# Splitting the two feed-forward weight loads of a Mamba2 + SwiGLU layer into six pieces with semaphores of their own

## What is computed

```python
xn = layernorm(x)
# attn branch: mixer (not shown), then a SwiGLU with float32 weights, 2752 wide
h  = xn + mamba2_mixer(rmsnorm(xn))
a  = h + (silu(rms(h) @ gate_w.T) * (rms(h) @ up_w.T)) @ down_w.T
# ffn branch: a SwiGLU with int32 weights scaled by 1/127, 3072 wide
f  = (silu(xn @ wg.T) * (xn @ wu.T)) @ wd.T
out = x + a + f
```

## Time and profile before

| | us |
|---|---|
| time, median of 2 runs | 4552.88 |
| the 2 runs | 4582.55 and 4523.2 |
| profiled execution, its own time | 4524.84 |
| its span, slowest core (core 5) | 4523.1 |
| spans of the 8 cores | 4493.2 to 4523.1 |
| PE busy in the span | 2282.1 (50%) |
| DVE busy in the span | 1812.8 (40%) |

### The profile page before, as it was taken

The page is one execution under the profiler, slowest core; times in us unless marked ns, Lnnn a source line. Parts: engine busy times, 40 slices in busy tenths (PEclk is TensorE's granted clock), DMA queues, the critical chain, the costliest instruction groups (busy, mean ns, idle before and its releaser), DMA issues.

```text
span 4523.1 us, 36356 instructions; the slowest of 8 cores (4493.2 to 4523.1 us)
## 1 busy us (share of the span) xinstructions
PE 2282.1 (50%) x9681; PEld 1012.9 (22%) x9681; DVE 1812.8 (40%) x3925; ACT 559.7 (12%) x1011; POOL 149.6 (3%) x152
## 2 busy tenths in 40 slices
PE   0526603438850334343433322777776706878877
PEld 0212201213320111111111111333333302333333
DVE  3532495653139565656565640222222201222222
ACT  3000020000122221212121110111111000000000
POOL 0110000000000000000000000000000000000000
PEclk9998755559975555555555556788888758988988
DMA  6552000011120311111111136000000081111111
GB/s 163 190 156 59 19 0 1 1 40 22 53 59 0 84 66 38 61 42 57 47 52 50 49 79 108 19 19 24 24 19 19 15 158 44 49 33 33 49 33 35
DMA packets 85968, 234.08 MB, mean 52 GB/s; under 512 B 23856, under 2 KB 24656, under 8 KB 85136
## 3 DMA queue, kind: packets, MB, share of 16 engines
q0 software_dynamic: 32128, 106.44, 10.2%
q1 hardware_dynamic: 51344, 116.94, 8.4%
q10 hardware_dynamic: 2304, 8.39, 0.5%
HBM read 235.13 MB, written 51.66 MB: 63 GB/s over the span
## 4 chain that ended last, share of the span: by engine, by line
PE 43%; DVE 21%; issue 15%; DMA 9%; ACT 5%; another core or an unknown queue 5%; DVEq 1%; SPq 0%; ACTq 0%; POOL 0%; POOLq 0%
PE P L1057 4%; PE P L1207 4%; PE P L1211 4%; PE P L930 3%; PE P L1061 3%; PE P L420 3%; PE P L425 3%; DMA bcast<-lam_dram 3%; DMA wbuf<-w_in 3%; DVE Emt L845 2%; PE P L1246 2%; PE P L1098 2%; PE PS L1246 2%; PE P L645 2%
## 5 line engine op out<-in xcount | busy, mean ns | idle before, releaser
L851 PE MATMUL P<-x_tok,Emt 128*128 128x64 bf16 x512 | 108.4, 212 | 293.8 <-DVE Emt L845 278.9
L549 DVE SCALAR_TENSOR_TENSOR B_acc<-xbc,c_convw,B_acc 128x2048 bf16<-128x2048 bf16 x108 | 245.3, 2344 | 0.0
L1228 DVE TENSOR_TENSOR F_h<-F_h,P 128x1024 bf16<-128x1024 bf16 x48 | 58.6, 1221 | 436.0 <-ACT F_h L1222 436.0
L1207 PE MATMUL P<-wg,F_xf 128*128 128x512 bf16 x384 | 146.3, 381 | 164.8 <-DMA wd2b<-w_d 119.9
L836 ACT ACTIVATE Est<-Est 128x128 f32<-128x128 f32 x512 | 156.5, 310 | 432.4 <-DVE Est L830 430.9
L332 PE MATMUL P<-c_identf,A_n 128*128 128x128 f32 x256 | 90.6, 445 | 197.9 <-DVE A_n L320 166.2
L1078 DVE TENSOR_TENSOR E_h<-E_h,P 128x1024 bf16<-128x1024 bf16 (+1 forms) x48 | 53.3, 1110 | 336.9 <-ACT E_h L1072 336.9
L1057 PE MATMUL P<-wg,E_hnT 128*128 128x512 bf16 x384 | 146.3, 404 | 65.8 <-ACT E_h L1072 65.4
L845 DVE SCALAR_TENSOR_TENSOR Emt<-Est,dtk,Gm 128x128 bf16<-128x128 f32 x512 | 175.8, 346 | 9.1 <-PE P L851 6.5
L830 DVE TENSOR_SCALAR Est<-bcast,lam_tok 128x128 f32<-128x128 f32 x512 | 152.5, 303 | 54.0 <-DMA bcast<-lam_dram 4.3
L645 PE MATMUL P<-c_identf,dt 32*128 32x32 f32 x32 | 8.9, 278 | 321.1 <-issue 161.5
(11 more groups left out here) (198 smaller groups left out, 4278.1 us busy)
## 6 DMA issues: line engine op xcount, KB each, us to landing
bcast<-lam_dram SPq DMA_DIRECT2D x64, 512.0 KB
A_x<-x_own SPq DMA_DIRECT2D x32, 512.0 KB, 3.8
A_x<-x_pre SPq DMA_DIRECT2D x32, 512.0 KB, 4.2
wd<-w_d POOLq DMA_DIRECT2D x2, 5376.0 KB, 102.9
xn_dram<-A_n POOLq DMA_DIRECT2D x16, 512.0 KB, 4.6
xfh<-xfp_dram SPq DMA_DIRECT2D x4, 2048.0 KB, 14.3
sz_dram<-zst POOLq DMA_DIRECT2D x32, 256.0 KB, 2.3
sz_t<-sz_dram POOLq DMA_DIRECT2D x16, 512.0 KB, 3.9
```

The source lines that it names most:

```text
L549: e.scalar_tensor_tensor(a[:, :], xbc[:, ec * CW + k:ec * CW + k + T], self.c["convw"][:, ec * 4 + k:ec * 4 + k + 1], a[:, :], ALU.mult, A ...
L1207: e.matmul(slots[j][:, 0:512], xft[p][:, dc * 128:(dc + 1) * 128], w[:, dc * INTER2 + cb:dc * INTER2 + cb + 512], start=(dc == 0), stop=(d ...
```

## The change

In both phases the loads of gate and up are split by the column parts that the matmuls use, and issued in the order in which tile 0 needs them: gate part 0, up part 0, gate part 1, and so on. These six loads take semaphores in turn from the list `dw, dl0, dl1, dp, dw, dl0`. A load whose semaphore is already in use makes GpSimd wait until the earlier load on it has landed. The down load follows on `dl1` and the rest of down on `dp`, with the same kind of wait. TensorE's wait at the head of the phase is gone. In its place, in tile 0 alone, each of the six gate and up groups waits for its own piece, and the first down matmul waits for both down loads. The bytes loaded and the places they go to stay the same. What computes stays the same.

The part for E; the one for F is the same with 3 parts of 1024 columns and the `wg2, wu2, wd2, wd2b` tiles:

```diff
-        ldg = self.op("gpsimd", lambda e: e.dma_start(
-            bass.AP(wg1, 0, [[NDC * INTER1, 128], [INTER1, NDC], [1, INTER1]]),
...
-            inc=("dw", 16), wait=[("st", self.cnt["st"])])
...
-        self.wait("tensor", "dw", lddb)
+        EPARTS = [(0, 1024), (1024, 1024), (2048, 704)]
+        wsem = ["dw", "dl0", "dl1", "dp", "dw", "dl0", "dl1", "dp"]
+        t_wg, t_wu = {}, {}
+        si = 0
+        first = [("st", self.cnt["st"])]
+        lastw = {}
+        for pi, (cb, cn) in enumerate(EPARTS):
+            for wdst, wsrc, td in ((wg1, self.w_g1, t_wg), (wu1, self.w_u1, t_wu)):
+                s = wsem[si]
+                w = first + ([(s, lastw[s])] if s in lastw else [])
+                tok = self.op("gpsimd",
+                    lambda e, wdst=wdst, wsrc=wsrc, cb=cb, cn=cn: e.dma_start(
+                        bass.AP(wdst, cb, [[NDC * INTER1, 128], [INTER1, NDC], [1, cn]]),
+                        bass.AP(wsrc.tensor, cb,
+                                [[INTER1, 128], [128 * INTER1, NDC], [1, cn]])),
+                    inc=(s, 16), wait=w)
+                td[pi] = (s, tok)
+                lastw[s] = tok
+                first = []
+                si = (si + 1) % len(wsem)
+        t_wd = ("dl1", self.op("gpsimd", lambda e: e.dma_start(
...
+            inc=("dl1", 16), wait=[("dl1", lastw["dl1"])]))
+        t_wdb = ("dp", self.op("gpsimd", lambda e: e.dma_start(
...
+            inc=("dp", 16), wait=[("dp", lastw["dp"])]))
...
                             wait=(([("sa", t_silu_u.get(uu - 1)), ("sv", t_hnt[i])]
-                                   if j == 0 else [("sv", t_spu.get(uu - 1))])
+                                   if j == 0 else [("sv", t_spu.get(uu - 1))]) +
+                                  ([(t_wg if j == 0 else t_wu)[pi]] if i == 0 else [])
                                   if dc == 0 else []),
...
-                        wait=([("sv", t_tr), ("sv", t_v1b.get(i - 1))]
+                        wait=([("sv", t_tr), ("sv", t_v1b.get(i - 1))] +
+                              ([t_wd, t_wdb] if i == 0 else [])
                               if k == 0 and q == 0 else []),
```

More of the change, by code:

```diff
@@ L1133, in phase_F @@
         h3t = cv("F_h3t", OFF["R_B"] + 22528, [128, 24 * 128], BF16)
[L1134 to L1142, removed]
+        wsem = ["dw", "dl0", "dl1", "dp", "dw", "dl0", "dl1", "dp"]
+        t_wg, t_wu = {}, {}
+        si = 0
+        first = [("st", self.cnt["st"])]
+        lastw = {}
+        for pi in range(3):
+            cb = pi * 1024
+            for wdst, wsrc, td in ((wg2, self.w_g2, t_wg), (wu2, self.w_u2, t_wu)):
+                s = wsem[si]
+                w = first + ([(s, lastw[s])] if s in lastw else [])
+                tok = self.op("gpsimd",
+                    lambda e, wdst=wdst, wsrc=wsrc, cb=cb: e.dma_start(
+                        bass.AP(wdst, cb, [[NDC * INTER2, 128], [INTER2, NDC], [1, 1024]]),
+                        bass.AP(wsrc.tensor, cb,
+                                [[INTER2, 128], [128 * INTER2, NDC], [1, 1024]])),
+                    inc=(s, 16), wait=w)
+                td[pi] = (s, tok)
+                lastw[s] = tok
+                first = []
+                si = (si + 1) % len(wsem)
+        t_wd = ("dl1", self.op("gpsimd", lambda e: e.dma_start(
             bass.AP(wd2, 0, [[21 * DM, 128], [DM, 21], [1, DM]]),
             bass.AP(self.w_d2.tensor, 0, [[DM, 128], [128 * DM, 21], [1, DM]])),
-            inc=("dw", 16))
-        lddb = self.op("gpsimd", lambda e: e.dma_start(
+            inc=("dl1", 16), wait=[("dl1", lastw["dl1"])]))
+        t_wdb = ("dp", self.op("gpsimd", lambda e: e.dma_start(
             bass.AP(wd2b, 0, [[3 * DM, 128], [DM, 3], [1, DM]]),
             bass.AP(self.w_d2.tensor, 21 * 128 * DM, [[DM, 128], [128 * DM, 3], [1, DM]])),
-            inc=("dw", 16))
-        self.wait("tensor", "dw", lddb)
+            inc=("dp", 16), wait=[("dp", lastw["dp"])]))
         slotA_b = P1[:, 640:704].bitcast(BF16)
@@ L1216, in phase_F @@
                                     ("de%d" % p, t_ldx[i])] if j == 0 else
[L1217 removed]
+                                   [("sv", t_spu.get(uu - 1))]) +
+                                  ([(t_wg if j == 0 else t_wu)[pi]] if i == 0 else [])
                                   if dc == 0 else []),
```

9 lines of the change are left out of this document (removed).

## The result

| | before | after |
|---|---|---|
| median of all executions (10 and 13) | 4580.0 | 4535.49 |
| profiled execution, its own time | 4524.84 | 4448.42 |
| undisturbed executions | 4523.2 to 4533.9 | 4448.4 to 4454.4 |

In most executions of both kernels the cores of one die (four of the eight) run at a lower TensorE clock and take longer, so all comparisons from here on are between the others, called undisturbed. Their ratio, after to before, is on record as 0.981 with a 95% interval of 0.976 to 0.986; the middles of the two groups, 4528 and 4452, give 0.983, about 75 us less. A later measurement of the changed kernel gave 0.983 (0.978 to 0.987). The kernel is faster than before, but whether by more than two per cent these intervals leave open, since both reach across 0.98.

The account below looks back on a forecast made before the run. The prediction took the head of each feed-forward phase to be bound by the bytes of the weight loads, with tile 0 waiting behind all of them. It summed 4524.84 - 47.2 - 36.8 = 4440.8, given as 4441 us, range 4420 to 4482.

Parts of the forecast that it names:

- the base: Whole kernel: the profiled execution before, 4524.84 us, from which the gains were subtracted; with the median as base, 4469.
- Last landings unchanged: Heads of E and F: bytes and pace stay, so the last weights land at 2783.6 and 3748.5 us as before.
- the short rows: E's 704-column pieces: cost by bytes, so nothing added; 7.7 us if a shorter row cost as much as a longer.
- The 47.2 us of E: Head of E: gain from the first down matmul starting at 2783.9 instead of 2831.10.
- The 36.8 us of F: Head of F: gain from the first down matmul starting at 3748.8 instead of 3785.56.
- From there each phase runs as today: After the first down matmul in E and F: the rest of each phase keeps its time.
- GpSimd's waits: Load issue in both heads: the queue never runs dry, so cost nothing; 12 us a phase if the cover were gone.
- the slack: Tile 0 of each phase: ready for down ahead of the down weights by 5.4 us in E and 11.2 in F.
- (a): Weight loads in both heads: short rows load faster, gains grow by 16 and 18 us, time 4407; chance 0.09.
- (b): Weight loads beside tile 0: VectorE's work holds them up, last landings slip by 21.4 us in all, 4462; chance 0.12.
- (c): Gate and up pieces: strided pieces load slower, the 84 us gain gone at 107 GB/s, 4541 at 100; chance 0.04.
- (d): Gate and up pieces: all complete near the end, tile 0 starts no earlier, nothing gained, 4525; chance 0.05.

Follow-up runs that it names:

- experiments 4: Changed kernel with each gate and up piece loaded as two loads of half the columns, same bytes, twice the rows; 4470.25 us.
- 10: Changed kernel plus F's gate loaded during E, E's last store issued from SyncE, and E's gate loaded whole with only up in three pieces; ratio 0.976 of before.
- experiment 3: Changed kernel with a semaphore of its own for each of the eight loads, so GpSimd waits for none of them; 4455.63 us.
- Experiment 7: Kernel before with its whole loads reordered, down first, then gate, then up, and TensorE waiting for up; 4531.83 us.

## Why the prediction was right and where it was wrong

The forecast was 4441 with a range of 4420 to 4482. The undisturbed executions took 4448 to 4454: inside the range and 7 to 13 us above the forecast. The median of all executions, 4535.49, lies outside it. A chance of 0.66 had been put on a ratio within two per cent of 1 and 0.32 on a faster kernel; 0.981 lies at this border, and its interval on both sides of it.

**The step that failed is the base.** The sum was made against one profiled execution of 4524.84, and I kept this as the base for the forecast too, though the median of the two runs shown was 28 us higher and one of them stood at 4582.55. The executions of before turned out to reach from 4523 to 4712 with a median of 4580.0, those of the changed kernel from 4448 to 4682: a scatter larger than the whole change. The range took in "some of the scatter", up to 4482; even the other base that the text works out, 4469, leaves 13 us above it for a scatter of which the shown runs already made 59. A better base alone would not have done: 4580.0 - 84 = 4496 is still 39 us below the median measured, because the changed kernel's median lies 83 us above its undisturbed executions and that of before only 52. The saving, forecast at 84 and measured at 75, had about the right size; the level to which it was applied had not.

**Last landings unchanged** held within 1.4 us in F and failed by 4.4 us in E. The failed term is the one for the short rows: "I take nothing, since the engines are held back by the shared memory and not by rows". The row behind it, the load of w_in at 212 GB/s, was read while the neighbour, core 4, moved 4 GB/s, and experiments 4 and 10 measured 16 to 20 ns a row with both cores loading. The bound kept for the range, 128 rows at 60 ns = 7.7 us, had the right size by luck: it was put on the rows of 704 columns, which run at 173 GB/s as before, while the delay came with the rows of 1024 columns, for which nothing was kept. A first look would have been a count of packets, which the transfer view gives.

**One core's stretch stood for all.** The 47.2 us of E are core 5's. From its last landing to its first down matmul there were 47.5 us; on the mean of the cores it was 146.5 - 101.1 = 45.4. Together with the 4.4 us of landing and 0.2 from landing to matmul that leaves 40.8. The 36.8 us of F met 36.2 on the mean, with two small misses that cancel: 37.8 us from landing to down before, and a landing 1.4 us later. But the time is that of the slowest core: after the change this is core 6, whose F head takes 118.6 us, where core 5's was forecast at 113.5. On the slowest cores the two heads gave 72.7 us instead of 84.0.

**"From there each phase runs as today"** held for the slowest cores, with 804 and 736 us. On the mean of the cores E's remainder grew by 5.4 us with the granted clock of its tiles, a term that the sum put at nothing. The prediction had named a change of the later tiles as a sign of being wrong.

**The steps that held.** GpSimd's waits cost nothing (experiment 3). TensorE's groups of gate and up each ended before the next piece: six waits per phase, all above zero. TensorE stood idle for 8.9 us (E) and 17.5 us (F) before the first down matmul, waiting for its weights; the slack was forecast at 5.4 and 11.2. In F the last up piece came 84.9 us after the first issue, 83.4 forecast; in E 78.2 instead of 71.9, as late against the forecast as this core's last landing (107.5 us, forecast 101.1). Beside the loads the clock was even granted better than the 1.2 GHz (0.50) that the sum used for a group, 0.77 from 2715 to 2740, which changed nothing, as the pieces set the pace.

**The rivals.** (a) Short rows load faster: out. Experiment 7 moved the 212 GB/s to the long rows, and the pieces land later, not sooner. (b) VectorE holds up the loads: out. With nothing computing beside them the pieces land at 106.1 us, with tile 0 beside them at 105.5. By the Trainium skill's "DVE blocks DMA" trap ("SBUF — State Buffer"), a two-port operation of VectorE keeps GpSimd from writing descriptors. If tile 0 had such operations, the landing with tile 0 beside the loads would be the later one; no run here shows such a loss. (c) Strided pieces load slower: right in sign, at 4.4 us and not 84. In E this fits the count of rows (experiments 4 and 10); F's 1.4 us for as many rows does not fit it. (d) The pieces land together: out, by the six waits. The first gate matmul came 20.1 us after the first issue in E and 22.0 in F, forecast some 18.

The lone pace of 212 GB/s written comes back in experiment 7 (215); the paired one lies between 155, for E's pieces of 1024 columns, and some 172. Twice 172 and 212 is 344 and 424 read. The Trainium skill ("HBM Reference", Specifications) gives about 358 and 425; the trace agrees for the lone core and stays 4% below for the paired one.

## What to carry to other kernels

When a phase starts behind a bulk load, first let each consumer wait for its own load; here that gave 72 of the 77 us of the two heads. Ordering pieces by need comes second and gave 5. Once tile 0 is ready before the last weights land, an earlier first transfer helps (some 18 to 25 us here), and a store that a barrier needs should not stand in the queue behind it. Cut loads no finer than the reserve asks, since added rows can cost (13 to 20 ns each on a transfer engine in E). Set the level of a forecast by all runs shown, not by the profiled one, and read what a change gave from the stretches that it touches.

## What the runs showed of the hardware

**The offset between neighbours sets the landing.** The two cores of a pair (0 and 1, 2 and 3, and so on) share the pace, so the one that starts later runs its tail alone at 212 GB/s. For F, means over the four pairs of one profile each:

| kernel | offset of first issues, us | last landing of F, us |
|---|---|---|
| E's rows padded (5) | 6.4 | 121.3 |
| split without waits (2) | 10.9 | 118.9 |
| down first, whole loads (7) | 12.2 | 117.6 |
| own semaphores (3) | 14.6 | 117.9 |
| changed kernel again (11) | 14.9 | 116.7 |
| changed kernel | 15.6 | 116.4 |
| before, whole loads | 17.7 | 115.0 |
| waits alone, whole loads (1) | 21.3 | 115.2 |

Over all these kernels, single pairs whose F phases start about 3 us apart land at 120 to 123 us on the mean of their two cores, those 27 to 32 us apart at 112 to 113. A straight line through the 32 pairs gives 0.35 us of landing for a us of offset in F, and 0.28 in E. The offsets of two executions of one kernel differ by some us, so a head's change of 1 us, as in F, can't be read without them. The 4.4 us of E are not of this kind: there the offset was 13.2 us before and 11.0 after, worth 0.6 us. At the same offset the six pieces land 3.4 us later than whole loads in E and 0.7 us later in F.

**A row has a price beside its bytes.** In E it was 13 to 20 ns for each row added on a transfer engine, in three comparisons: 13 from whole loads to six pieces at the same offset (3.4 us for 260 rows), 16 for halved rows, 20 for a whole gate. Both cores of a pair were loading, and the shared pace seemed to be the limit. In the F head the split paid only about 1 us for 260 rows, though halving the rows there once more cost 6.5. That difference stays open.

**The granted clock moves a tile of E by 3 us.** At 0.83 a tile took 51 us, at 0.78 it took 54, in the same kernel and on the same core. What decides between the two is not shown here.
